# Two fused transformer layers: the attention stage's order of steps, with row scores further ahead and two engines' subtractions set apart

## The reference, cut to what matters

```python
qkv = x @ W_qkv.T + b_qkv
q, k, v = split(qkv, 3), each reshaped to (2, 1024, 16 heads, 32)
scores = einsum('bqhe,bkhe->bhqk', q, k) / sqrt(32)
scores = where(causal, scores, -inf)
attn = softmax(scores, axis=-1)
out = einsum('bhqk,bkhe->bqhe', attn, v)
```

## Time and profile before

| What | Value |
|---|---|
| Median of three runs | 1739.25 us (1739.24 to 1741.14) |
| The profiled execution's own time | 1735.57 us |
| Its span, first to last instruction | 1733.7 us |
| TensorE busy over the span | 1661.0 us (96%) |
| VectorE, ScalarE, GpSimd busy | 1018.7, 655.5, 557.8 us |
| Mean granted TensorE clock | 0.985 |
| Attention stage, in the span's time | about 769 to 1157 us |

### The profile page before, as it was taken

The page is one execution under the profiler, slowest core; times in us unless marked ns, Lnnn a source line. Parts: engine busy times, 40 slices in busy tenths (PEclk is TensorE's granted clock), DMA queues, the critical chain, the costliest instruction groups (busy, mean ns, idle before and its releaser), DMA issues. The chain is left out here.

```text
span 1733.7 us, 21900 instructions
## 1 busy us (share of the span) xinstructions
PE 1661.0 (96%) x7804; PEld 1295.1 (75%) x7804; DVE 1018.7 (59%) x1667; ACT 655.5 (38%) x1271; POOL 557.8 (32%) x540
## 2 busy tenths in 40 slices
PE   5999999999999999999989989989999999999998
PEld 3676888788788877876656656658888888888887
DVE  4321365564623454358988989855655555555785
ACT  4421322232213332228878878762222222222221
POOL 4201210310310003117777767672144031033320
PEclk9999999999999999989999999999999999999999
DMA  7200210110101038843554545323010010012243
GB/s 287 102 12 1 61 49 19 55 31 20 60 7 37 25 108 250 291 170 75 121 120 106 122 112 133 79 73 129 0 52 25 1 49 25 1 49 71 76 133 134
DMA packets 101916, 141.80 MB, mean 82 GB/s; under 512 B 43881, under 2 KB 52713, under 8 KB 100274
## 3 DMA queue, kind: packets, MB, share of 16 engines
q1 hardware_dynamic: 100946, 134.05, 26.4%
q10 hardware_dynamic: 864, 6.39, 1.2%
HBM read 93.74 MB, written 46.53 MB: 81 GB/s over the span
## 5 line engine op out<-in xcount | busy, mean ns | idle before, releaser
L1538 ACT ACTIVATE prob<-p_turn 128x512 f32<-128x512 f32 (+3 forms) x384 | 176.2, 487 | 56.9 <-PE p_turn L1510 36.9
L1577 DVE TENSOR_TENSOR pt_lo<-prob,pt_hi 128x512 fp32r<-128x512 f32 (+3 forms) x256 | 173.7, 703 | 33.7 <-ACT pt_hi L1546 33.2
L1570 DVE TENSOR_REDUCE row_top<-p_score 128x1 fp32r<-128x128 f32 (+7 forms) x256 | 184.6, 746 | 14.4 <-PE p_score L1494 12.5
L1025 DVE TENSOR_TENSOR hid<-hid,p_up 128x512 f32<-128x512 f32 x64 | 44.0, 687 | 218.2 <-PE p_up L490 202.5
L1593 POOL TENSOR_TENSOR pt_lo<-prob,pt_hi 128x512 fp32r<-128x512 f32 (+1 forms) x128 | 167.0, 1305 | 10.7
L1924 DVE TENSOR_TENSOR e_hid<-e_hid,e_p_up 128x512 f32<-128x512 f32 x64 | 44.0, 687 | 196.4 <-PE e_p_up L1819 196.4
L1524 PE MATMUL p_o<-pt_hi,v 128*65 128x512 f32 (+3 forms) x384 | 137.9, 362 | 3.9 <-POOL pt_lo L1593 2.3
L1590 POOL TENSOR_SCALAR pt_hi<-prob 128x512 fp32r<-128x512 f32 (+1 forms) x128 | 100.9, 788 | 106.3 <-ACT prob L1538 64.2
L1525 PE MATMUL p_o<-pt_lo,v 128*65 128x512 f32 (+3 forms) x384 | 128.5, 341 | 0.0
L1546 ACT ACTIVATE pt_hi<-prob 128x512 fp32r<-128x512 f32 (+3 forms) x256 | 120.6, 486 | 3.2 <-PE p_o L1525 0.2
L772 ACT ACTIVATE hid<-p_gate 128x512 f32<-128x512 f32 x64 | 38.3, 599 | 218.7 <-PE p_gate L490 218.6
(11 more groups left out here) (279 smaller groups left out, 4256.7 us busy)
## 6 DMA issues: line engine op xcount, KB each, us to landing
stack<-qk_parked SPq DMA_DIRECT2D x66, 256.0 KB, 4.9
raw<-in_wgu SPq DMA_DIRECT2D x64, 256.0 KB, 2.7
qk_parked<-qk SPq DMA_DIRECT2D x16, 1024.0 KB, 4.0
v_parked<-v_out SPq DMA_DIRECT2D x16, 520.0 KB, 7.4
o_parked<-o_both SPq DMA_DIRECT2D x64, 128.0 KB
stack_third<-qk_parked SPq DMA_DIRECT2D x30, 256.0 KB, 4.4
v<-v_parked ACTq DMA_DIRECT2D x6, 1040.0 KB, 8.3
res<-in_x SPq DMA_DIRECT2D x8, 512.0 KB
```

Source lines behind the costliest of these rows:

```text
L1538: act.activation(prob[:, n % PB, c0:W], p_turn[:, n % TB, c0:W], ACT.Exp).then_inc(exped, 1)
L1570: dve.tensor_reduce(top[:, h % 2, r:r + 1], p_score[:, r % 2, 0:width_of(r)], AX_X, ALU.max, negate=True).then_inc(topped, 1)
L1577: dve.tensor_tensor(pt_lo[:, n % PT, c0:W], prob[:, n % PB, c0:W], pt_hi[:, n % PT, c0:W].bitcast(F32), ALU.subtract).then_inc(split, 1)
```

## The change

The change replaces the table `ORDER` and nothing else. The scores 5, 6 and 7 of the row scores go from one head ahead to two, so that all eight are two heads ahead of the head that is being weighed; the reductions and the transfers of their results go with them. Each engine's list is written in a new order. GpSimd's list is the same. In SyncE's list the stack load goes from sixth to fourth place; before it stand place(7, 1), place(0, 2) and store(0, 0). TensorE's list now begins with score(0, 2). VectorE's list has rest(2) and rest(3) first, behind rest(0) of the iteration before.

```diff
@@ -1368,22 +1368,22 @@
     AHEAD = 2
     OWN = (1, 4, 6, 8)
     ORDER = {
-        "tensor": [("weigh", 0, 0), ("weigh", 1, 0), ("score", 5, 1), ("weigh", 2, 0), ("weigh", 3, 0), ("turned", 6, 0),
-                   ("score", 6, 1), ("turned", 7, 0), ("turned", 8, 0), ("weigh", 4, 0), ("weigh", 5, 0), ("score", 7, 1),
-                   ("score", 0, 2), ("turned", 9, 0), ("turned", 10, 0), ("turned", 11, 0), ("weigh", 6, 0),
-                   ("weigh", 7, 0), ("turned", 0, 1), ("score", 1, 2), ("score", 2, 2), ("turned", 1, 1),
-                   ("turned", 2, 1), ("weigh", 8, 0), ("weigh", 9, 0), ("score", 3, 2), ("weigh", 10, 0),
-                   ("weigh", 11, 0), ("score", 4, 2), ("turned", 3, 1), ("turned", 4, 1), ("turned", 5, 1)],
-        "scalar": [("exp", 3, 0), ("exp", 4, 0), ("round", 3, 0), ("exp", 5, 0), ("round", 5, 0), ("read_o", 0, 0),
-                   ("exp", 6, 0), ("exp", 7, 0), ("exp", 8, 0), ("round", 7, 0), ("exp", 9, 0), ("exp", 10, 0),
-                   ("round", 9, 0), ("exp", 11, 0), ("round", 10, 0), ("round", 11, 0), ("exp", 0, 1),
-                   ("round", 0, 1), ("exp", 1, 1), ("exp", 2, 1), ("round", 2, 1), ("read_o", 1, 0)],
-        "vector": [("top", 4, 1), ("rest", 2, 0), ("rest", 3, 0), ("top", 5, 1), ("rest", 5, 0), ("top", 6, 1),
-                   ("rest", 7, 0), ("top", 7, 1), ("top", 0, 2), ("rest", 9, 0), ("top", 1, 2), ("top", 2, 2),
-                   ("rest", 10, 0), ("rest", 11, 0), ("rest", 0, 1), ("top", 3, 2)],
+        "tensor": [("score", 0, 2), ("turned", 6, 0), ("weigh", 0, 0), ("weigh", 1, 0), ("weigh", 2, 0), ("weigh", 3, 0),
+                   ("turned", 7, 0), ("turned", 8, 0), ("score", 1, 2), ("score", 2, 2), ("weigh", 4, 0), ("turned", 9, 0),
+                   ("weigh", 5, 0), ("score", 3, 2), ("turned", 10, 0), ("score", 4, 2), ("weigh", 6, 0),
+                   ("turned", 11, 0), ("score", 5, 2), ("weigh", 7, 0), ("turned", 0, 1), ("turned", 1, 1),
+                   ("weigh", 8, 0), ("turned", 2, 1), ("turned", 3, 1), ("score", 6, 2), ("weigh", 9, 0),
+                   ("weigh", 10, 0), ("weigh", 11, 0), ("turned", 4, 1), ("turned", 5, 1), ("score", 7, 2)],
+        "scalar": [("exp", 5, 0), ("exp", 6, 0), ("round", 5, 0), ("read_o", 0, 0), ("exp", 7, 0), ("exp", 8, 0),
+                   ("round", 7, 0), ("exp", 9, 0), ("round", 9, 0), ("exp", 10, 0), ("round", 10, 0), ("exp", 11, 0),
+                   ("round", 11, 0), ("exp", 0, 1), ("exp", 1, 1), ("round", 0, 1), ("exp", 2, 1), ("exp", 3, 1),
+                   ("round", 2, 1), ("round", 3, 1), ("read_o", 1, 0), ("exp", 4, 1)],
+        "vector": [("rest", 2, 0), ("rest", 3, 0), ("top", 7, 1), ("top", 0, 2), ("rest", 5, 0), ("top", 1, 2),
+                   ("top", 2, 2), ("top", 3, 2), ("rest", 7, 0), ("top", 4, 2), ("top", 5, 2), ("rest", 9, 0),
+                   ("rest", 10, 0), ("rest", 11, 0), ("top", 6, 2), ("rest", 0, 1)],
         "gpsimd": [("divide", 4, 0), ("divide", 6, 0), ("divide", 8, 0), ("divide", 1, 1)],
-        "sync": [("place", 4, 1), ("store", 0, 0), ("place", 5, 1), ("place", 6, 1), ("place", 7, 1),
-                 ("stack", 2, 0), ("place", 0, 2), ("place", 1, 2), ("place", 2, 2), ("place", 3, 2), ("store", 1, 0)],
+        "sync": [("place", 7, 1), ("place", 0, 2), ("store", 0, 0), ("stack", 2, 0), ("place", 1, 2), ("place", 2, 2),
+                 ("place", 3, 2), ("place", 4, 2), ("place", 5, 2), ("place", 6, 2), ("store", 1, 0)],
     }
```

## The result

The changed kernel takes 1792.82 us (median of 4 runs, 1789.53 to 1795.33), the kernel before 1740.2 (4 runs, 1739.24 to 1741.59): a ratio of 1.0301, 95% interval 1.0282 to 1.0320. It is **slower by 3%** where the forecast was 1.7% faster; what rival 4 describes came, 28.5 us beyond its 1764.3. The profiled execution took 1792.72, its span 1790.9.

A forecast was written before the change was run, and what follows sets the result against it. TensorE was held up by late row-top transfers, their clock drops, and VectorE's subtractions. First head read at 795.0, plus 303.1 for 29 heads, 9.1 stack-load wait and 19.6 at the end: 29.6 less, so 1709.6 us; range 1696 to 1727.

The forecast's parts named there:

- rival 4: Stack load's third transfer regularly lands 8.3 after issue; score(0) waits 2.9 every second head, clock drops; 1764.3 us, chance 0.08.
- (a): Attention stage, scores further ahead: turned scores' waits for row tops and both clock drops go; worth 22.8 us.
- (b): VectorE's subtractions kept apart from GpSimd's: three quarters of 1.6 us a head saved, head period 10.45; at most 16 us.
- Rival 2: Attention heads: ScalarE and GpSimd wait for each other, another chain keeps the period at 10.97; 1717.5 us, chance 0.20.
- Rival 3: The port shared by VectorE and GpSimd is the bound, a head takes 11.3; 1725 us, chance 0.06.
- (c): Stack load on SyncE lands about 11.1 into the iteration; score(0) waits 0.65 in 14 heads, costing 9.1 us.
- (d): Attention stage's edges: opening costs +1.5 us (bounds 0 and +3); last two head periods take 19.6 instead of 20.5.

The follow-up runs named there:

- e15: Changed kernel with the stack load one place earlier on SyncE, before store(0,0), and each store issued as two transfers of 32 rows; 1702.70 us, ratio 0.9780.
- e12: e9 with one more GpSimd subtraction of 512 columns, on a tile of its own, directly behind divide(1,1); 1746.51 us.
- e13: Changed kernel, order untouched, with each store issued as two transfers of 32 rows; 1740.38 us, ratio 1.0014.
- e6: Changed kernel with both stores moved behind the stack load in SyncE's list; 1736.41 us, ratio 0.9979.
- e9: e6 with the load of the values issued a step later, at the next head's read_o(0); 1729.67 us, ratio 0.9937.
- e5: Changed kernel with store(0,0)'s 128 KB transfer issued a second time, to a tensor of its own, directly ahead of the stack load; 1825.78 us.
- e8: e6 with VectorE's rest(2) and rest(3) put back behind top(7,1); 1776.88 us.

## Why the prediction was wrong

**(a) right.** All row tops in time but one; the waits of the earlier trace rows went from 27.5 to 1.2, and e15, which has no long waits at score(0) that could hide them, has none. The two drops they caused went with them.

**(b) right in sign and in its result.** Quick heads take 10.33, forecast 10.45, and the weighs' waits for VectorE are gone (VectorE is busy 9.77 of a quick head, forecast 9.5). The mean of 0.55 that I gave for the subtractions was too low: it is 0.646. I took three quarters of the 1.6 of waiting as saved, 1.2 a head; in the quick heads the eight subtractions sum to 5.0 instead of 5.8, so it was 0.8. The period did not hang on that size, since TensorE is now busy all of a quick head (10.40 of 10.40). No run tells how much of the gain comes of the subtractions and how much of the scores' lead. Rival 2 is out: no other chain holds 10.97. Rival 3 is out too: by an estimate from the rows of both kernels GpSimd's four subtractions (1.28 three times, 1.01) and four copies (0.6 each) and VectorE's 4.0 take 11.3 one after the other, and a head takes 10.33. The rule of the Trainium skill (SBUF — State Buffer, Who interferes with whom) that the prediction weighed does describe the direction: e12 shows that GpSimd's work beside VectorE's subtractions stretches them by 40%. Its "whole instruction" is more than these heads show, as the earlier trace rows had it.

**(c) wrong: the step that failed.** I put the third transfer's landing at 6.1 after its own issue, that is 11.1 into the iteration, and the wait at 0.65 in 14 heads, 9.1 in all. Measured: the third lands 9.0 after its own issue in the median (8.1 to 10.4). Counted from the first: issue at 4.5 to 5.1, once at 9.0 (I had 3.9; place(7, 1), the first in SyncE's list, goes out only when top(7) is done, 2.5 into the iteration, and in 5 of the 14 place(0, 2) waits for the landing of the previous head's place(3) as well), landing 9.8 behind it, at 14.8 in the median; the waits are 63.6 in 14 heads. The number was read from loads of the kernel before, where three row tops stand between store and load. I moved the load next to the store and kept the landing of its old place. The prediction names the store ahead of the load, but only for its 0.5 of issue; what its transfer does to those behind it had no term. Its own upper bound, 8.3, was one row of the old place too, and most of the measured landings pass it.

**Rival 4 had the mechanism,** with a gap at score(0) and a drop behind it, and put the odd heads at 15.0; they take 16.2 to 17.7. Its wait was 2.9 and is 4.5; its drop 3.4 long, and is 6.8. Given 0.08, it deserved more: the margin of (c) was negative already in the forecast, and the price came from one load's row.

**(d)** In this pair of traces the start costs 5.6, not 1.5. The stage's opening runs at the lower level for 20.5 us instead of 17.0, beginning at 771.3 instead of 768.7:

```profile
771.30:791.80 20.50, 19.79 (x63) 12.81 (x63) 15.09 (x21) 6.36 (x13) 6.92 (x7) 0.50 0.16 39
```

The lower level ends 6.1 later than in the earlier trace rows. Much of that is not the change's: e13, with the same list for TensorE, opens with 17.0 at the lower level and reads its first head at 795.9, so some 3.2 of the 5.6 go with the longer stretch and 2.4 remain. Over all traces the first head is read at 798.6 on average with the scores further ahead (14 traces, 794.6 to 801.5) and at 794.6 without (4 traces, 790.2 to 798.7). The last two periods took 19.6, as forecast.

So the sum: my 1709.6 lacks 4.1 at the opening, 54.5 of waiting at score(0) (63.6 less 9.1), and 14 x 2.2 = 31 of clock behind it; from this the quick heads' 0.12 in 29 (3.5) goes off again. That makes about 1796 against the measured 1792.8. The last 3.7 are those that I added because the median of the kernel before lay that far above its profiled execution; in the changed kernel the two are equal.

## What to carry to other kernels

The landing time of a transfer belongs to its place in the queue, not to the transfer: when a load moves, price it by what is issued directly ahead of it, and look at how that neighbour spreads over the DMA engines. A tail in which few engines work while the consumer waits is a reason to change the neighbour before looking for bandwidth. And where the first step of an in-order engine's iteration hangs on such a load with no lead to spare, count its bound, and the clock's echo, as a case of weight.

## What the runs showed of the hardware

- **A store of two outer blocks works on few DMA engines.** Its 64 rows of 2 KB, written as two blocks of 32, leave a queue tail at 16% of the engines; as two transfers of 32 rows the following load lands 2.7 us sooner (7.1 against 9.8, e13). The Trainium skill (DMA: Bandwidth & Descriptors, Why a DMA increments its semaphore by 16 and not by 1) says that a transfer issued by SyncE or ScalarE uses the largest number of engines up to 16 that divides the slowest dimension on both sides. By that rule the store, 2 blocks on one side and 64 rows on the other, has 2 engines and its halves have 16 each; the trace agrees for the store: its 64 packets of 2 KB take 86 ns each and some 2.7 us together, so two go out at once. For the halves it shows eight at once (0.52 of the engines in e13), not 16. I did not weigh this rule in the prediction.
- **Small transfers wait behind large ones of another engine's queue.** Row tops of 0.5 KB issued by SyncE land up to 12.7 into the iteration instead of 4.2 to 8.5 behind ScalarE's 1040 KB (e6). Being issued first does not save them: one issued 1.7 us ahead of that load lands 11.4 after its issue (e9).
- **The clock followed every long wait.** Fourteen waits of 3.2 us and more, fourteen drops to 1.2 GHz of 6.8 us; at e13's waits of about 2.2 nine drops, most of 3.4. Each drop followed TensorE's standing still. Its length goes with the wait only roughly: seven of e5's eight waits of 6.9 and more were followed by 10.2 to 13.7, but in e13 one wait of 2.5 was followed by no drop, and in e8 waits of 1.2 were followed by drops of 3.4.
- **Open** is why the stack load still takes 6.2 to 7.1 with the stores out of its way, and why the value load catches a row top of every eighth head alone in e9.
